# Rows 1 to 3 of Wo split in steps 6, 10 and 15 of a group, and the last Q tile evicted behind the transposes of P

## The chip, the cores and the metric

The kernel runs on one core of a Trainium2 chip. The metric is the device time of one execution in microseconds (us). TensorE is called PE here, VectorE DVE, ScalarE ACT, GpSimd POOL and SyncE SP; SP only issues DMAs.

## What is computed

The reference is one gated cross-attention layer and one gated feed-forward layer over 16 batches of 128 tokens of width 1024, in float32:

```python
q = (layernorm(x) @ Wq)                      # 32 heads of 32
k, v = ctx_4096 @ Wk, ctx_4096 @ Wv          # 8 heads of 32, 4 query heads share one
attn = softmax(q k^T / sqrt(32))
x = x + tanh(g_xattn) * ((attn v) @ Wo)
x = x + tanh(g_ffn) * (silu(layernorm(x) @ W_gate.T) * (layernorm(x) @ W_up.T)) @ W_down.T
```

## The kernel before

Every large product is made of three matmuls on 32-bit operands: each operand is split into a high part, which ACT writes by a rounding copy (L730), and a low part, the difference, which DVE writes (L1059). Weights, P, Q and the attention output all go through such a pair, ACT first and DVE behind it.

The attention works in 4 groups (g) of 4 batches, 512 tokens each. Within a group a program order is written out by hand in steps n = 0 to 37; in the first 32 of them (UNITS = 32) there is one unit of scores each: the scores of one batch and four heads. The steps are not synchronised; they only give the order of each engine's queue. In step n:

- PE (L1618 to L1644) makes the scores of unit n, one quarter of a Q tile (`q_part(n + 2)`, 6 matmuls, while n < 22; the 8 Q tiles are i = 0 to 7, and tile 7 is finished in step 21), the transposes of P of unit n - 3, from step 22 to step 29 one part of the output product with Wo (`o_part`), and in even steps from 6 on the product of P with V of pair m = (n - 6) / 2 (`weigh_values`, L1560), 12 matmuls.
- ACT (L805 to L820) evicts the output of pair m (`o_out`, odd n from 7, m = (n - 7) / 2), the transposed P of unit n - 3 (`pt_out`), computes the exponentials of unit n (`exps`, 4 activations), evicts a Q tile in steps 2, 6, 10, ..., 22 (`q_out`, two activations of 64 rows), and then copies the high part of a column tile of the weights (COL_STEP) or of a row of Wo (ROW_STEP), if one is due in this step.
- DVE (L1200 to L1218) takes the row maxima of unit n, inverts the sums of unit n - 1, makes the low part of a Q tile in steps 3, 7, ..., 23, the low part of the weights that ACT split one step before, the low part of the output of a pair (`o_out`), and the low part of P (`pt_out`).
- POOL multiplies P by the inverted sums (L624), and builds the block form of V (L594).
- SP (L377) issues the loads in an order of its own, each behind the wait for its buffer.

`weigh_values` of pair m waits for the low part of the output of pair m - 1 (`o_lo`, L1563 to L1564), since both use PSUM bank 5. The scores of units 24 and above read the last Q tiles: unit 25 is the first that needs tile 7, and so does `o_part(0, 3, 1)` in the same step, whose PSUM bank it was in.

A row of Wo goes through one buffer, `wr_raw`: SP loads row i once the low part of row i - 1 is made (`load_wr`, L340). Four rows (0 to 3) are ready before the output product of the group begins, rows 4 to 7 follow after the steps. `place_keys(g, 1, c)` (L360) is 12 DMAs of 32 KB that copy the keys of the second half of the heads into the block form `kb_h`, `kb_l`; c = 0 is needed by the scores of unit 16 (L1536), c = 1 by those of unit 20. In SP's queue `place_keys(g, 1, 0)` stands behind the loads of column tiles 8 and 9 (L386, L387), and the load of row 2 of Wo behind `place_keys(g, 1, 0)`.

After the attention come two halves of the feed-forward layer (from 700 us on), which the change does not touch.

Of the kernel before, what the change touches and what calls it, by code (L numbers as in the profile page):

```python
# [23 lines left out]
NQ = D // P  # L24
# [6 lines left out]
UNITS = NB * NH * GQ  # L31
# [3 lines left out]
STEPS = UNITS + 5  # L35

COL_STEP = {5: 0, 6: 5, 7: 9, 8: 32, 9: 33}
ROW_STEP = {0: 1, 1: 13, 2: 17, 3: 21}
KB_DMAS = 12 * 16


# [43 lines left out]
def gated_cross_attention_ffn(nc, x, ctx_t, wc, wr, wf, wm, wd, g_xattn, g_ffn, x1d, hd, out):  # L85

    with ExitStack() as ctx:
# [201 lines left out]
        def wcn(g, i):  # L289
            return g * NC + (NKV + i)  # L290
# [43 lines left out]
        def _(sp):  # L334
            def load_wc(g, i):

                sp.wait_ge(wc_lo, wcn(g, i) - 1)
                sp.dma_start(wc_raw[:, i % 2, :], wc[i]).then_inc(wc_in[i % 2], 16)

            def load_wr(g, i):  # L340

                if i > 0:
                    sp.wait_ge(wr_lo, g * NO + i)
                sp.dma_start(wr_raw[:, :], wr[i]).then_inc(wr_in, 16)
# [15 lines left out]
            def place_keys(g, a, c):  # L360
                if a == 0:
                    sp.wait_ge(kb_zero, g + 1)
                    sp.sem_inc(passed, 1)
                    sp.wait_ge(k_lo, g * NB + (2 * c + 2))
                else:
                    sp.wait_ge(s_done, g * UNITS + (8 + 4 * c + 4))
                two = slice(2 * c, 2 * c + 2)
                for j in range(4):
                    src, cols = slice(j * HD, (j + 1) * HD), slice(j * P, (j + 1) * P)
                    kl = kc_l[src, a, 2 * c * P:(2 * c + 2) * P].rearrange("p (b k) -> p b k", b=2)  # L370
                    kh = kc_h[src, a, 2 * c * P:(2 * c + 2) * P].rearrange("p (b k) -> p b k", b=2)
                    sp.dma_start(kb_l[src, two, cols].bitcast(F32), kl.bitcast(F32)).then_inc(kb_in[c], 16)
                    for half in range(2):
                        rows = slice(half * H2 + j % 2 * HD, half * H2 + j % 2 * HD + HD)
                        sp.dma_start(kb_h[rows, two, cols].bitcast(F32), kh.bitcast(F32)).then_inc(kb_in[c], 16)

            def body(g, last):  # L377
                load_wc(g, 4)
                load_wr(g, 0)
                load_wc(g, 5)  # L380
                place_keys(g, 0, 1)
                load_wc(g, 6)
                load_wr(g, 1)
                load_wc(g, 7)
                if not last:
                    load_wc(g, 8)  # L386
                    load_wc(g, 9)  # L387
                place_keys(g, 1, 0)
                load_wr(g, 2)
                place_keys(g, 1, 1)  # L390
                load_wr(g, 3)
                load_wr(g, 4)
                if last:
                    sp.wait_ge(wc_used, NG * NQ)
                    sp.wait_ge(x1_out, 16 * 8 + 1)
                    sp.dma_start(xa[:, :, :], x1d[0:NB].rearrange("t p n -> p t n")).then_inc(xa_in, 16)
                    sp.dma_start(xb[:, :, :], x1d[NB:2 * NB].rearrange("t p n -> p t n")).then_inc(xb_in, 16)
                    load_fraw(0, 0, 0)
                sp.wait_ge(pt_done, g * UNITS + UNITS)
                for i in (5, 6, 7):  # L400
                    sp.dma_start(wl_raw[:, :] if i == 7 else wo_raw[:, i - 5, :], wr[i]).then_inc(wo_in[i - 5], 16)
                if not last:
                    load_xn(g, 0)
                    load_xn(g, 1)
                    load_wc(g, 10)
                    load_wc(g, 11)
                sp.wait_ge(pv_done, g * PAIRS + PAIRS)
                if not last:
                    for b in range(2):
                        load_ct(g + 1, b, ctx_t[bass.ds(g * NB + (NB + b), 1), :, :].rearrange("o p n -> (o p) n"))  # L410
                src = x[g * NB:(g + 1) * NB] if last else x[bass.ds(g * NB, NB), :, :]
                sp.dma_start(x1[:, :, :], src.rearrange("t p n -> p t n")).then_inc(x1_in, 16)
                if not last:
                    for b in range(2, NB):
                        load_ct(g + 1, b, ctx_t[bass.ds(g * NB + (NB + b), 1), :, :].rearrange("o p n -> (o p) n"))
                if not last:
                    load_wc(g + 1, 0)
                    load_wc(g + 1, 1)
                for n, t in enumerate(LAST_ORDER if last else range(NB)):
                    sp.wait_ge(x1_add, g * YN + (2 * n + 2))  # L420
                    if not last and n in (1, 2):
                        load_xn(g, n + 1)
                    dst = x1d[g * NB + t] if last else x1d[bass.ds(g * NB + t, 1), :, :].rearrange("o p n -> (o p) n")
                    sp.dma_start(dst, x1[:, t, :]).then_inc(x1_out3 if last and t == NB - 1 else x1_out, 16)
                if not last:
                    load_wc(g + 1, 2)
                    load_wc(g + 1, 3)
# [142 lines left out]
            for g in range(NG - 1):  # L570
                body(g, False)
# [156 lines left out]
        def _(act):  # L728
# [69 lines left out]
            def body(g, last):  # L798
                kt_out(g, 3)
                split_wc(g, 4)  # L800
                q_out(g, 0)
                q_out(g, 1)

                act.wait_ge(x1_out, g * (16 * NB) + 1)
                for n in range(STEPS + 1):  # L805
                    if n >= 7 and n % 2 == 1:
                        o_out(g, (n - 7) // 2)
                    if 3 <= n < UNITS + 3:
                        pt_out(g, n - 3)
                    if n < UNITS:  # L810
                        exps(g, n)
                    if n % 4 == 2 and n < UNITS - 8:
                        q_out(g, n // 4 + 2)

                    for i in COL_STEP:
                        if COL_STEP[i] == n and not (last and i >= NQ):
                            split_wc(g, i)
                    for i in ROW_STEP:
                        if ROW_STEP[i] == n:
                            split_wr(g, i)  # L820

                for e in range(4):
                    act.wait_ge(o_first, g * 4 + (e + 1))
                    split_wr(g, 4 + e)
                if not last:
                    G = g + 1
                    split_wc(g, NQ + 2)
                    split_wc(g, NQ + 3)
                    split_ct(G, 0)
                    split_ct(G, 1)  # L830
                    kv_out(G, 0)
                    split_ct(G, 2)
                    split_wc(G, 0)
                    kv_out(G, 1)
                    split_ct(G, 3)
                    kt_out(G, 0)
                    xt_out(G, 0)
                    xt_out(G, 1)
                    split_wc(G, 1)
                    kv_out(G, 2)  # L840
                    kt_out(G, 1)
                    xt_out(G, 2)
                    xt_out(G, 3)
                    kv_out(G, 3)
                    kt_out(G, 2)
                    split_wc(G, 2)
                    split_wc(G, 3)
# [208 lines left out]
        def _(dve):  # L1056
# [136 lines left out]
            def body(g, last):  # L1193
# [6 lines left out]
                for n in range(STEPS + 1):  # L1200
                    if n < UNITS:
                        row_max(g, n)
                    if 1 <= n < UNITS + 1:
                        invert(g, n - 1)

                    if n % 4 == 3 and n < UNITS - 8:
                        q_out(g, n // 4 + 2)
                    for i in COL_STEP:
                        if COL_STEP[i] + 1 == n and not (last and i >= NQ):
                            split_wc(g, i)  # L1210
                    for i in ROW_STEP:
                        if ROW_STEP[i] + 1 == n:
                            split_wr(g, i)
                    if n >= 7 and n % 2 == 1:
                        m = (n - 7) // 2
                        o_out(g, m)
                    if 3 <= n < UNITS + 3:
                        pt_out(g, n - 3)  # L1218
                if last:
                    dve.wait_ge(rs2, 1)  # L1220
                    dve.wait_ge(xa_in, 16)
                    dve.wait_ge(xb_in, 16)
                    for t in range(NB - 1):
                        normalise_first(t)
# [688 lines left out]
```

## Time and profile before

| what | us |
|---|---|
| median of 3 runs | 2035.76 |
| lowest and highest of them | 2034.85 to 2037.85 |
| the profiled execution, its own time | 2039.46 |
| its span, first to last instruction | 2037.7 |
| attention, groups 0 to 3 with what lies before | 0 to about 700 |

The granted clock of TensorE is 0.997 of full speed over the span. Times of the trace are counted from the start of the span. A matmul in the trace has a modelled length that reaches over the start of the next one, so what a wait costs PE is read from the distance between starts. A row of the timeline gives start, length, engine, line, operation, output <- inputs and form; behind it stands the idle time before it and what ended that.

### The profile page before, as it was taken

The page shows a single profiled execution, that of the slowest core. Times are in us where ns is not written, and L with a number is a line of the kernel's source. Part 1 is how long each engine was busy: PE and PEld are TensorE (multiplying, and loading weights), DVE is VectorE, ACT ScalarE, POOL GpSimd, SP SyncE. Part 2 cuts the span into 40 slices and gives each one's busy share as a digit, 9 for nine tenths or more (in the row PEclk, how much of TensorE's full clock was granted, in tenths as well). Part 3 has the DMA queues.
Part 4 walks back from the last instruction along what each step waited for, and adds up shares of the span by engine and source line. Part 5 has one row for each costly group of instructions (what it writes and reads, how often), then busy time and mean ns, then how long its engine had stood idle before and what let it go on. Part 6 is the DMA issues. An engine that isn't in the chain of part 4 may idle for free.

```text
span 2037.7 us, 29091 instructions
## 1 busy us (share of the span) xinstructions
PE 1998.2 (98%) x9800; PEld 1677.5 (82%) x9800; DVE 1224.3 (60%) x1818; ACT 913.2 (45%) x2218; POOL 653.4 (32%) x601
## 2 busy tenths in 40 slices
PE   8999999999999999999999999999999999999999
PEld 6888888888888888888888878777888888888877
DVE  7767776776776864545543655574544545444455
ACT  4873683586387443333333434343333333233334
POOL 2440441242244554544542201023454454300000
PEclk9999999999999999999999999999999999999999
DMA  5225215324424222212213576763222222256676
GB/s 199 82 91 191 90 49 210 118 58 161 143 60 173 89 83 93 92 62 93 93 62 127 188 253 189 239 207 104 82 93 75 79 93 79 87 171 207 209 237 220
DMA packets 90634, 266.49 MB, mean 131 GB/s; under 512 B 11184, under 2 KB 37296, under 8 KB 85168
## 3 DMA queue, kind: packets, MB, share of 16 engines
q1 hardware_dynamic: 90256, 264.81, 38.8%
q8 instruction: 51, 0.84, 0.2%
q10 hardware_dynamic: 288, 0.52, 0.1%
q14 instruction: 39, 0.32, 0.0%
HBM read 221.25 MB, written 39.32 MB: 128 GB/s over the span
## 4 chain that ended last, share of the span: by engine, by line
PE 87%; DVE 7%; ACT 4%; issue 1%; DMA 0%; DVEq 0%; SPq 0%; ACTq 0%
PE ps L1507 27%; PE ps L1508 27%; PE ps L1509 27%; ACT pb L787 2%; PE ps L1557 2%; PE ps L1549 1%; PE ps L1548 1%; DVE wc_l L1059 1%; DVE qo_l L1095 1%; DVE qo_h L1095 1%; DVE kb_h L1109 1%; ACT wc_h L730 1%; DVE xo L1405 1%; PE ps L1602 1%; DVE dl L1059 1%
## 5 line engine op out<-in xcount | busy, mean ns | idle before, releaser
L1507 PE MATMUL ps<-xop_h,w_h 128*128 128x512 f32 x1208 | 473.2, 392 | 3.0 <-issue 3.0
L1508 PE MATMUL ps<-xop_l,w_h 128*128 128x512 f32 x1208 | 471.2, 390 | 0.0
L1509 PE MATMUL ps<-xop_h,w_l 128*128 128x512 f32 x1208 | 471.1, 390 | 0.0
L1507 PE MATMUL ps<-dh,hh 128*128 128x512 f32 x672 | 265.1, 394 | 6.3 <-DVE xo L1405 5.1
L1507 PEld LDWEIGHTS ps<-xop_h,w_h 128*128 128x128 f32 x1208 | 227.5, 188 | 50.3 <-issue 3.4
L1509 PEld LDWEIGHTS ps<-xop_h,w_l 128*128 128x128 f32 x1208 | 227.4, 188 | 47.3
L1508 PEld LDWEIGHTS ps<-xop_l,w_h 128*128 128x128 f32 x1208 | 227.5, 188 | 46.6
L1509 PE MATMUL ps<-dh,hl 128*128 128x512 f32 x672 | 261.9, 390 | 0.0
L1508 PE MATMUL ps<-dl,hh 128*128 128x512 f32 x672 | 261.9, 390 | 0.0
L1059 DVE TENSOR_TENSOR w_l<-fraw,w_h 128x512 fp32r<-128x512 f32 x130 | 129.4, 996 | 213.5 <-ACT w_h L730 213.5
L730 ACT ACTIVATE w_h<-fs 128x512 fp32r<-128x512 f32 x168 | 105.7, 632 | 292.5 <-PE ps L1509 281.7
L1059 DVE TENSOR_TENSOR dl<-dr,dh 128x1024 fp32r<-128x1024 f32 (+1 forms) x132 | 170.9, 1294 | 46.5 <-ACT dh L730 46.4
L624 POOL TENSOR_TENSOR pb<-pb,rinv 128x512 f32<-128x512 f32 x128 | 133.2, 1041 | 202.1 <-DVE rinv L1119 202.1
L787 ACT ACTIVATE pb<-ps,nmx 128x128 f32<-128x128 f32 x512 | 182.7, 389 | 18.3 <-DVE nmx L1114 17.8
L694 POOL TENSOR_TENSOR hb<-hb,cc 128x512 f32<-128x512 f32 x42 | 54.2, 1290 | 405.0 <-ACT hb L914 400.4
L730 ACT ACTIVATE hh<-hr 128x384 fp32r<-128x384 f32 (+1 forms) x132 | 64.5, 489 | 260.1 <-PE ps L1509 254.7
L1059 DVE TENSOR_TENSOR hl<-hr,hh 128x384 fp32r<-128x384 f32 (+1 forms) x126 | 72.2, 573 | 146.4 <-ACT hh L730 146.3
L1507 PEld LDWEIGHTS ps<-dh,hh 128*128 128x128 f32 x672 | 126.4, 188 | 35.0 <-DVE dl L1059 6.8
L1509 PEld LDWEIGHTS ps<-dh,hl 128*128 128x128 f32 x672 | 126.3, 188 | 26.5
L1508 PEld LDWEIGHTS ps<-dl,hh 128*128 128x128 f32 x672 | 126.4, 188 | 24.6
L730 ACT ACTIVATE dh<-dr 128x1024 fp32r<-128x1024 f32 x132 | 138.2, 1047 | 4.0 <-DMA dr<-in_wd 4.0
L1059 DVE TENSOR_TENSOR w_l<-fs,w_h 128x512 fp32r<-128x512 f32 x168 | 138.0, 823 | 1.6 <-ACT w_h L730 1.6
(161 smaller groups left out, 3856.3 us busy)
## 6 DMA issues: line engine op xcount, KB each, us to landing
dr<-in_wd SPq DMA_DIRECT2D x132, 512.0 KB, 4.3
fraw<-in_wf SPq DMA_DIRECT2D x42, 1024.0 KB, 5.4
wc_raw<-in_wc SPq DMA_DIRECT2D x44, 512.0 KB, 4.3
hd<-hb SPq DMA_DIRECT2D x42, 512.0 KB, 2.9
hr<-hd SPq DMA_DIRECT2D x84, 192.0 KB, 2.9
wr_raw<-in_wr SPq DMA_DIRECT2D x20, 512.0 KB, 3.6
x<-in_x SPq DMA_DIRECT2D x4, 2048.0 KB, 11.4
x1d<-x SPq DMA_DIRECT2D x16, 512.0 KB, 4.8
```

Source lines behind the costliest of these rows:

```text
L624: nc.gpsimd.tensor_tensor(p, p, r, ALU.mult).then_inc(normed, 1)
L694: nc.gpsimd.tensor_tensor(hb[:, 1, :], hb[:, 1, :], cc[:, 1, :], ALU.mult).then_inc(h_ready, 1)
L730: return nc.scalar.activation(out, in_, ACT.Copy, scale=scale)
L787: ins = nc.scalar.activation(pb[:, n % 4, j * P:(j + 1) * P], ps[:, n % 3, j * P:(j + 1) * P], ACT.Exp, bias=nmx[:, n % 4, j:j + 1], accum ...
L1059: return nc.vector.tensor_tensor(out, whole, hi.bitcast(F32), ALU.subtract)
L1095: ins = nc.vector.scalar_tensor_tensor(q[others, i, :], ps[rows, q_bank(i), :], SCALE, q[rows, i, :].bitcast(F32), ALU.mult, ALU.subtract)
L1109: ins = nc.vector.tensor_copy(kb_h[rows, b, cols], kc_h[src, 0, keys].bitcast(F32))
L1405: nc.vector.scalar_tensor_tensor(place, ps[:, Y_BANK[p][idx], :], tg[:, 1:2], place, ALU.mult, ALU.add).then_inc(y_free, 1)
L1507: pe.matmul(out, w_hi_, m_h, start=first, stop=False, skip_group_check=goes_on)
L1508: pe.matmul(out, w_hi_, m_l, start=False, stop=False, skip_group_check=goes_on)
L1509: return pe.matmul(out, w_lo_, m_h, start=False, stop=last, skip_group_check=goes_on)
L1557: ins = pe.transpose(ps[:, 3 + n % 2, j * P:(j + 1) * P], pb[:, n % 4, j * P:(j + 1) * P], ident[:, :])
```

## The change

Three things are moved; nothing is added or removed.

```diff
-ROW_STEP = {0: 1, 1: 13, 2: 17, 3: 21}
+ROW_STEP = {0: 1, 1: 6, 2: 10, 3: 15}
...                                          SP, body
                 load_wr(g, 1)
                 load_wc(g, 7)
+                load_wr(g, 2)
                 if not last:
                     load_wc(g, 8)
                     load_wc(g, 9)
+                load_wr(g, 3)
                 place_keys(g, 1, 0)
-                load_wr(g, 2)
                 place_keys(g, 1, 1)
-                load_wr(g, 3)
                 load_wr(g, 4)
...                                          ACT, step n
                     if 3 <= n < UNITS + 3:
                         pt_out(g, n - 3)
+                    if n == UNITS - 9:
+                        q_out(g, NQ - 1)
                     if n < UNITS:
                         exps(g, n)
-                    if n % 4 == 2 and n < UNITS - 8:
+                    if n % 4 == 2 and n < UNITS - 10:
                         q_out(g, n // 4 + 2)
...                                          DVE, step n
-                    if n % 4 == 3 and n < UNITS - 8:
+                    if n % 4 == 3 and n < UNITS - 9:
                         q_out(g, n // 4 + 2)
...
                     if 3 <= n < UNITS + 3:
                         pt_out(g, n - 3)
+                    if n == UNITS - 9:
+                        q_out(g, NQ - 1)
```

ACT splits the rows 1, 2, 3 in steps 6, 10, 15 and DVE makes their low parts in steps 7, 11, 16; before it was 13, 17, 21 and 14, 18, 22. Q tile 7 is evicted by ACT in step 23 between `pt_out` and `exps`, before it was the end of step 22; by DVE at the end of step 23, before it was ahead of `o_out` and `pt_out` of step 23. On SP the loads of rows 2 and 3 now stand ahead of `place_keys(g, 1, 0)`.

## Rows read from the trace of the kernel before

**Rows 1.** The page: busy time, share of the span, instructions

```profile
PE 1998.2 (98%) x9800; PEld 1677.5 (82%) x9800; DVE 1224.3 (60%) x1818; ACT 913.2 (45%) x2218; POOL 653.4 (32%) x601
```

**Rows 2.** Waits of PE (us in total, times, longest), whole span

```profile
PE ps L1507 <- DVE qo_l L1059: 9.4, 12, 1.4
```

**Rows 3.** Timeline of PE, end of steps 8 and 10 of group 1

```profile
242.49 0.60 PE L1557 MATMUL ps<-ident,pb 128*128 128x128 f32 x4
243.59 0.36 PE L1507 MATMUL ps<-pt_h,vp_h 128*128 128x256 f32 x1 [0.51 <-DVE qo_l L1059]
...
249.28 0.60 PE L1557 MATMUL ps<-ident,pb 128*128 128x128 f32 x4
249.63 0.36 PE L1507 MATMUL ps<-pt_h,vp_h 128*128 128x256 f32 x1
```

**Rows 4.** Timeline of DVE, step 7 of group 1

```profile
242.30 0.69 DVE L1095 SCALAR_TENSOR_TENSOR qo_l<-ps,qo_l 64x512 fp32r<-64x512 f32 x1
243.02 0.42 DVE L1059 TENSOR_TENSOR qo_l<-ps,qo_h 128x256 fp32r<-128x256 f32 x1
```

**Rows 5.** Timeline of ACT in step 9, DVE in 11, PE in 12, group 1

```profile
247.61 0.60 ACT L730 ACTIVATE pt_h<-ps 128x512 fp32r<-128x512 f32 x1 [1.15 <-PE ps L1557]
...
254.94 0.43 DVE L1059 TENSOR_TENSOR qo_l<-ps,qo_h 128x256 fp32r<-128x256 f32 x1
...
255.67 0.36 PE L1507 MATMUL ps<-pt_h,vp_h 128*128 128x256 f32 x1
```

**Rows 6.** DVE's low parts of rows 0 to 4: count, ns min/median/max

```profile
L1059 DVE TENSOR_TENSOR wr_l<-wr_raw,wr_h x20: 1226/1432/1980, 59.3 to 666.5; 128x1024 fp32r<-128x1024 f32 x20
```

**Rows 7.** Timeline of POOL and DVE in steps 3 and 7 of group 1

```profile
228.74 1.04 POOL L624 TENSOR_TENSOR pb<-pb,rinv 128x512 f32<-128x512 f32 x1 [1.84 <-DVE rinv L1119]
228.89 1.98 DVE L1059 TENSOR_TENSOR wr_l<-wr_raw,wr_h 128x1024 fp32r<-128x1024 f32 x1 [0.23 <-ACT wr_h L730]
...
241.49 1.04 POOL L624 TENSOR_TENSOR pb<-pb,rinv 128x512 f32<-128x512 f32 x1 [0.98 <-DVE rinv L1119]
```

**Rows 8.** Timeline of ACT and DVE, steps 21 to 23 of group 1

```profile
285.71 1.08 ACT L730 ACTIVATE wr_h<-wr_raw 128x1024 fp32r<-128x1024 f32 x1
286.66 0.62 ACT L730 ACTIVATE pt_h<-ps 128x512 fp32r<-128x512 f32 x1
...
288.50 0.61 ACT L730 ACTIVATE qo_h<-ps 64x512 fp32r<-64x512 f32 x1
289.74 0.38 ACT L730 ACTIVATE qo_h<-ps 128x256 fp32r<-128x256 f32 x1
...
289.75 0.68 DVE L1095 SCALAR_TENSOR_TENSOR qo_h<-ps,qo_h 64x512 fp32r<-64x512 f32 x1 [0.21 <-ACT qo_l L730]
291.17 0.42 DVE L1059 TENSOR_TENSOR qo_l<-ps,qo_h 128x256 fp32r<-128x256 f32 x1
```

**Rows 9.** Timeline of PE, step 24 and the start of 25, group 1

```profile
288.65 0.28 PE L1549 MATMUL ps<-kb_l,qo_l 128*128 128x256 f32 x1
289.00 0.63 PE L1557 MATMUL ps<-ident,pb 128*128 128x128 f32 x4
289.93 0.40 PE L1509 MATMUL ps<-wr_h,qo_l 128*128 128x512 f32 x1
291.74 0.36 PE L1507 MATMUL ps<-pt_h,vp_h 128*128 128x256 f32 x1 [1.41 <-DVE qo_l L1059]
293.24 0.28 PE L1548 MATMUL ps<-kb_h,qo_h 128*128 128x256 f32 x1
```

**Rows 10.** SP's issues before step 16, landing of `kb_h` (min/median/max), unit 16's scores

```profile
252.41 0.60 SPq L372 DMA_DIRECT2D kb_l<-kc_l  x1
258.80 1.24 SPq L375 DMA_DIRECT2D kb_h<-kc_h  x2
...
DMA to landing us min/median/max: 1.9/1.9/3.2
...
265.45 0.36 PE L1548 MATMUL ps<-kb_h,qo_h 128*128 128x256 f32 x1
```

## Prediction, made before the changed kernel was run

> **What bounds the kernel.** I read the page first, then the table of PE's waits, then PE's timeline by the distance between starts. The page shows PE busy for 98% of the span [rows 1]: the time is PE's queue plus the holes in it. Most work is feed-forward, which the change doesn't touch, so only holes of the attention can move. The waits show that in the attention PE has practically one releaser, DVE's `qo_l`, 12 times, 9.4 us [rows 2]: three places, the same in each of the four groups. They are:
>
> - Step 8, ahead of `weigh_values(1)`: from the start of the transposes to its first matmul it is 243.59 - 242.49 = 1.10 us, where step 10 has 249.63 - 249.28 = 0.35 [rows 3]. The hole is 0.75 us.
> - Step 24, ahead of `weigh_values(9)`: 291.74 - 289.93 = 1.81 us after the last matmul of `o_part`, whose successor comes 0.23 us later where nothing waits, so 1.58; in the same step the transposes come 0.35 us after the last matmul of the scores instead of 0.12, another 0.23 [rows 9]. Together 1.81 us.
> - Step 32, about half a microsecond: DVE's `o_out` stands there behind row maxima which wait for PE's own scores. It is tied to PE and moves with it; the change leaves it alone.
>
> **The change, part by part.** All times are those of group 1.
>
> *What goes: the hole of step 24.* In the old order ACT copies row 3 of Wo at 285.71, the last thing of step 21; the copy takes 0.95 us of ACT's queue (the next operation follows 0.95 us later), and so the exponentials of unit 22, and behind them Q tile 7 at 288.50, come late. DVE does this tile from 289.75 and only behind it the `o_out` of pair 8 at 291.17, whose end, 291.17 + 0.42 = 291.59, releases PE 0.15 us later at 291.74 [rows 8, 9]. The new order takes 0.95 us out of ACT ahead of it, and puts `o_out` and `pt_out` of step 23 ahead of the tile on both engines. ACT's `o_out(8)` then starts where the tile did, less the copy: 288.50 - 0.95 = 287.55. DVE makes it behind the row maxima of unit 23, which follow PE; it ends by about 288.9, and `weigh_values(9)`, without any hole due at 291.74 - 1.81 = 289.93, finds it done. The hole of 0.23 goes too: its transposes waited for a low part of P that stood behind the low part of row 3. Gain 1.81 us.
>
> What is late next is tile 7 itself. ACT: from 287.55 `o_out` and `pt_out`, 0.38 and 0.62 long; an ACT operation starts 0.13 before the end of the one ahead (285.71 + 1.08 against 286.66), so they take 0.74 and the tile is copied from 288.29, two halves in 1.24 (288.50 to 289.74) to 289.53. DVE: two halves in 1.42 (289.75 to 291.17) to 290.96, and PE could go on at 291.11. The scores of unit 25 are due 1.50 us (293.24 - 291.74) after `weigh_values(9)`, at 289.93 + 1.50 = 291.43 [rows 8, 9]. It fits by 0.32 us. This is the thinnest cover in the sum; if it were gone, each tenth of a microsecond beyond is one tenth lost per group.
>
> *What comes: row 1 in step 7 of DVE.* The low part of row 1 now stands between the Q tile of step 7 and `o_out(0)`, that is, directly ahead of the operation for which PE already waits in step 8. `o_out(0)` starts at 243.02, right behind the tile [rows 4]. ACT's copy of row 1, 1.08 long, starts when ACT has done its part of the Q tile, and so does DVE's part of the tile, which takes 1.42 [rows 8]: the copy is ready first and adds nothing. The shortest low part takes 1.226 us [rows 6]; the next operation starts 0.08 us before its end, so 1.15 us are put in. The hole of 0.75 becomes 1.90. The trace of before has no such split in this place. From below, it costs nothing if DVE had room there, which the rows exclude: the tile and `o_out` are back to back. From above, the longest of the 20 took 1.98 [rows 6], so 1.90. I take 1.15, since the long one at 228.89 began while POOL's multiply of 228.74 was running, whereas POOL's multiply of this step runs from 241.49 to 242.53 and is over before 243.02 [rows 7].
>
> The Trainium skill says why ("SBUF — State Buffer", section "Who interferes with whom"): a DVE instruction with two SBUF inputs and a GpSimd instruction that reads SBUF exclude each other, and the one that issues second blocks. The trace agrees: 228.74 + 1.04 + 1.23 = 231.01, the long split ended at 230.87. By this rule both new places are free of POOL; if one took the median of 1432 ns instead, the sum below would grow by 2 x 0.2 x 4 = 1.6 us.
>
> *Row 2 in step 11 of DVE.* The same order one period later: the low part stands between the Q tile and `o_out(2)`. That one started at 254.94, ended at 255.37 and would have let PE go at 255.52; `weigh_values(3)` started at 255.67 without a hole [rows 5]. So 0.15 of the 1.15 is covered and 1.00 is a new hole. Bounds: nothing, and 1.90 - 0.15 = 1.75; I take 1.00 for the same reason as above. By then the shift of step 8 has moved all queues alike: after each of these holes ACT and DVE stand ahead of PE again within two steps, because in step 9 of the old trace ACT sat idle for 1.15 us ahead of its `pt_out`, waiting for PE [rows 5], and likewise in step 13.
>
> *Row 3 in step 16 of DVE, rows 1 and 2 gone from 14 and 18.* Step 16 is even: behind the split come only `pt_out` and the next row maxima. The old order had the same split in steps 14 and 18, which are even too, and PE has no wait there [rows 2]. Nothing gained, nothing lost; from above, a split that meets POOL lasts 0.75 us more and still fits.
>
> *SP's queue.* The 12 DMAs of `place_keys(g, 1, 0)` started at 252.41 and the last was issued at 258.80 + 0.62 = 259.42, 7.01 us later [rows 10]. Now the load of row 3 stands ahead of them and waits for the low part of row 2. That ends, in old times plus the 1.15 of step 8, at 254.94 + 1.15 + 1.23 = 257.32. So: row 3 issued at 257.35, keys from 257.73, the last at 264.74, landed 1.9 us later at 266.64; with the longest landing of 3.2 at 267.94 [rows 10]. PE wants them at 265.45 + 1.15 + 1.00 = 267.60. Hidden by 0.96 us, in the worst case late by 0.34. `place_keys(g, 1, 1)` has no such gate and is needed four steps later. The loads of rows 2 and 3 themselves have over 6 us each until ACT wants them. In the last group row 4 and with it `x` for the feed-forward part are loaded sooner, but nothing reads them before the steps are over, so this is worth nothing.
>
> **Sum.** Per group +1.15 + 1.00 - 1.58 - 0.23 = +0.34 us, four groups +1.4 us. The profiled execution had a span of 2037.7 and a time of 2039.46; it would become 2039.1 and 2040.8. Its time lies 3.7 us above the median of the runs, so on the median: 2035.76 + 1.4 = 2037.1 us.
>
> **Rivals.**
>
> - *The new splits are hidden, and only the gain is seen:* -1.81 x 4 = -7.2, 2028.5 us. For it: DVE is busy only 60% of the span [rows 1], and ACT has idle time in step 9 [rows 5]. Against it: the releaser of the hole in step 8 is named, and the split stands directly ahead of it [rows 3, 4].
> - *POOL takes the splits:* if the low parts of rows 1 and 2 fall on POOL's multiply, each takes 1.98 as at 228.89, +1.90 + 1.75 - 1.81 = +1.84 per group, +7.4, 2043.1 us. It decides once DVE's split starts less than about 0.2 us after POOL's start; against it, 0.49 us lie between POOL's end and the split [rows 4, 7].
> - *The keys come late:* unit 16 of each group waits for a DMA. If the twelve issues take 0.6 us longer and land in 3.2, it is 0.34 + 0.6 = 0.94 per group, 3.8 in all, with the sum 2040.9 us. For it: a new gate ahead of the keys; against it: the median landing leaves 0.96 us [rows 10].
> - *Tile 7 is late:* the scores of unit 25 wait instead of `weigh_values(9)`. If it comes 0.7 us later than worked out, 0.37 per group, 1.5 in all, 2038.6 us.
>
> **How the numbers follow.** The forecast gets 0.50, the first rival 0.17, POOL 0.12, the keys 0.11, tile 7 0.10. The likeliest case and the last rival stay within 0.2% (4.1 us, about what a measurement of this kernel can tell from no change), as does a part of the keys' case, and those of partial cover on either side: faster 0.18, same 0.62, slower 0.20. The range reaches down towards the first rival and up to just short of POOL's: 2030.5 to 2042.5; the forecast's own is 2035 to 2039.5.
>
> **What would show it.** In the profile after: the wait of PE on `qo_l` in step 8 grows to about 1.7 us as listed (0.51 before), one of about 1 us appears in step 12, the one of 1.4 in step 24 is gone, the one of step 32 stays. The waits on `qo_l` are 12 again. DVE's `wr_l` of steps 7 and 11 take 1.23. SP's keys start 5 us later in the group, and PE lists no wait for a DMA of `kb_h`. The prediction is wrong if step 8 or 12 show no longer hole, if `wr_l` takes near 2 us there, or if unit 16 or unit 25 has a wait of its own.

## The result

| | before | after |
|---|---|---|
| median, 20 runs each | 2037.75 us | 2040.15 us |
| lowest to highest | 2034.85 to 2041.3 | 2038.66 to 2044.26 |
| profiled execution, its time and its span | 2039.46, 2037.7 | 2039.48, 2037.7 |

The ratio of the runs is 1.0017, 95% interval [1.0011, 1.0023]: the changed kernel is slower by 3.5 us, between 2.2 and 4.7; the two medians alone differ by 2.4. I had forecast 1.4 us more. The reader is to see three things in the profile after: both new holes are there, the old one is gone, and one of the rivals came true in one group of four. Engine busy times and PE's waits, from the page and the table of waits (us in total, times, longest):

```profile
PE 1995.8 (98%) x9800; PEld 1677.1 (82%) x9800; DVE 1228.0 (60%) x1818; ACT 914.0 (45%) x2218; POOL 649.1 (32%) x601
```

```profile
PE ps L1511 <- DVE qo_l L1061: 12.1, 12, 1.8
PE ps L1552 <- issue: 0.3, 1, 0.3
```

The waits on `qo_l` are 12 as in [rows 2], but 12.1 us instead of 9.4 (L1061 and L1511 are L1059 and L1507 of before). A second row has appeared, the scores' wait on nothing that the profile names.

Step 8 of group 1, PE's timeline, then DVE's of step 7:

```profile
243.37 0.60 PE L1561 MATMUL ps<-ident,pb 128*128 128x128 f32 x4
245.75 0.35 PE L1511 MATMUL ps<-pt_h,vp_h 128*128 128x256 f32 x1 [1.78 <-DVE qo_l L1061]
...
243.19 0.69 DVE L1097 SCALAR_TENSOR_TENSOR qo_l<-ps,qo_l 64x512 fp32r<-64x512 f32 x1
243.92 1.23 DVE L1061 TENSOR_TENSOR wr_l<-wr_raw,wr_h 128x1024 fp32r<-128x1024 f32 x1
245.18 0.42 DVE L1061 TENSOR_TENSOR qo_l<-ps,qo_h 128x256 fp32r<-128x256 f32 x1
```

The low part of row 1 stands between the Q tile and `o_out(0)`, and PE goes on 0.15 us after `o_out` ends (245.60). From the transposes to `weigh_values(1)` it is 2.38 us where [rows 3] had 1.10: 1.28 more. In step 11 and 12 the same picture, DVE first:

```profile
257.08 1.23 DVE L1061 TENSOR_TENSOR wr_l<-wr_raw,wr_h 128x1024 fp32r<-128x1024 f32 x1
258.34 0.42 DVE L1061 TENSOR_TENSOR qo_l<-ps,qo_h 128x256 fp32r<-128x256 f32 x1
...
258.91 0.35 PE L1511 MATMUL ps<-pt_h,vp_h 128*128 128x256 f32 x1 [0.85 <-DVE qo_l L1061]
```

From `weigh_values(1)` to `weigh_values(3)` it is 258.91 - 245.75 = 13.16 us, before 255.67 - 243.59 = 12.08 [rows 3, 5]: 1.08 more. Step 24 of PE, and Q tile 7 on DVE:

```profile
291.88 0.28 PE L1553 MATMUL ps<-kb_l,qo_l 128*128 128x256 f32 x1
292.00 0.60 PE L1561 MATMUL ps<-ident,pb 128*128 128x128 f32 x4
293.13 0.28 PE L1511 MATMUL ps<-pt_h,vp_h 128*128 128x256 f32 x1
294.56 0.28 PE L1552 MATMUL ps<-kb_h,qo_h 128*128 128x256 f32 x1
...
291.29 0.40 DVE L1061 TENSOR_TENSOR qo_l<-ps,qo_h 128x256 fp32r<-128x256 f32 x1
293.47 0.69 DVE L1097 SCALAR_TENSOR_TENSOR qo_l<-ps,qo_l 64x512 fp32r<-64x512 f32 x1
```

No hole is left: from the last matmul of the scores of unit 24 to the first of unit 25 it is 2.68 us, before 293.24 - 288.65 = 4.59 [rows 9], a gain of 1.91. `o_out(8)` is done at 291.69, well ahead. Tile 7 ends at 294.16, so PE could go on at 294.31, and the scores begin at 294.56: it fits by 0.25 us.

A period of a group, from the wait of step 32 in group 1 to that in group 2, sums it up; the row of each kernel, before and then after:

```profile
308.40 0.36 PE L1507 MATMUL ps<-pt_h,vp_h 128*128 128x256 f32 x1 [0.40 <-DVE qo_l L1059]
478.01 0.36 PE L1507 MATMUL ps<-pt_h,vp_h 128*128 128x256 f32 x1 [0.40 <-DVE qo_l L1059]
```

```profile
309.70 0.36 PE L1511 MATMUL ps<-pt_h,vp_h 128*128 128x256 f32 x1 [0.40 <-DVE qo_l L1061]
479.73 0.35 PE L1511 MATMUL ps<-pt_h,vp_h 128*128 128x256 f32 x1 [0.41 <-DVE qo_l L1061]
```

169.61 us became 170.03: 0.42 more (1.28 + 1.08 - 1.91 = 0.45, the rest is rounding of starts).

**The keys.** In group 0, and only there, unit 16 waits. SP first, then PE:

```profile
87.76 0.33 SPq L344 DMA_DIRECT2D wr_raw<-in_wr  x1
88.13 0.60 SPq L372 DMA_DIRECT2D kb_l<-kc_l  x1
94.54 2.17 SPq L375 DMA_DIRECT2D kb_h<-kc_h  x2
...
97.75 0.60 PE L1561 MATMUL ps<-ident,pb 128*128 128x128 f32 x4
98.66 0.35 PE L1552 MATMUL ps<-kb_h,qo_h 128*128 128x256 f32 x1 [0.31 <-issue]
```

The keys start behind the load of row 3, at 88.13, and the last pair of issues takes 2.17 us where all pairs ahead of it take 1.24. The scores come 0.91 us after the transposes instead of 0.35: 0.56 us lost. The profile calls it "issue", not DMA; that it is the keys is shown below. The pair is one issue of 1.53 us, at 94.54, and one of 0.60, at 96.11. The second, the last that unit 16 needs, also landed later than its like, 2.5 us after its issue. Of that DMA alone:

```profile
DMA to landing us min/median/max: 2.5/2.5/2.5
```

The last one in group 1 was issued at 265.76 and took 1.9. The scores were due at 97.75 + 0.35 = 98.10. By these numbers, with the long issue alone the last key would have landed at 96.11 + 1.9 = 98.0, just in time; both together made the wait.

**Why the two profiled spans are equal.** Four groups at 0.42 and 0.56 for the keys are 2.2 us, yet both spans are 2037.7. The stretches show it (length, busy of each engine, PEclk, DMA): before, then after.

```profile
584.00:596.00 12.00, 12.00 (x81) 10.75 (x81) 9.07 (x18) 10.59 (x42) 5.63 (x9) 1.00 0.07 18
1300.00:1400.00 100.00, 91.66 (x393) 73.69 (x392) 65.74 (x80) 42.89 (x66) 18.91 (x12) 0.95 0.59 200
```

```profile
584.00:596.00 12.00, 10.22 (x60) 9.32 (x60) 7.71 (x14) 8.81 (x40) 4.38 (x7) 0.86 0.16 45
1300.00:1400.00 100.00, 92.44 (x409) 74.65 (x408) 69.35 (x83) 43.87 (x68) 19.39 (x12) 0.98 0.62 208
```

The granted clock fell to its lower level, 1.2 GHz, for short stretches in both (a granted share of 0.50 from 1382 to 1384 before, and from 588 to 590 after): before only between 1300 and 1400, after there for a shorter time and once between 584 and 596. By these shares full clock would have given back about (1 - 0.95) x 100 = 5 us before, and (1 - 0.86) x 12 + (1 - 0.98) x 100 = 3.7 us after. The distances between starts say where it went. Two instructions of DVE that both kernels have, one behind the attention and one behind 1400, before and then after:

```profile
743.51 0.69 DVE L1322 TENSOR_TENSOR cc<-ps,x1c 128x512 f32<-128x512 f32 x1 [1.29 <-PE ps L1509]
1421.35 0.69 DVE L1322 TENSOR_TENSOR cc<-ps,x1c 128x512 f32<-128x512 f32 x1 [1.29 <-PE ps L1509]
```

```profile
747.12 0.69 DVE L1326 TENSOR_TENSOR cc<-ps,x1c 128x512 f32<-128x512 f32 x1 [1.29 <-PE ps L1513]
1421.37 0.69 DVE L1326 TENSOR_TENSOR cc<-ps,x1c 128x512 f32<-128x512 f32 x1 [1.29 <-PE ps L1513]
```

Behind the attention the changed kernel is 3.61 us late, and behind 1400 it is 0.02 us late. Of the 3.61, 1.5 are the low clock in group 3: its period, from the wait of step 32 in group 2 to that in group 3, is 1.90 us longer than before (651.22 - 479.73 against 647.60 - 478.01), the period shown above only 0.42. So 2.1 us are the change, and the feed-forward part, which the change does not touch, gave back 3.6 where the clock was low for longer before (by the shares 5 - 2 = 3 of them). One pair of profiles can't settle a change of this size by its spans; the distances between starts in stretches at full clock can.

### The profile page after: what moved, and what is told of

The parts are those of the page before. It is cut to its first block, busy times and chain, and to the rows that moved or that the text cites. A ratio compares the mean times of both kernels' runs of the same rounds, so it can differ in the third digit from the quotient of the medians.

```text
span 2037.7 us, 29091 instructions
## 1 busy us (share of the span) xinstructions
PE 1995.8 (98%) x9800; PEld 1677.1 (82%) x9800; DVE 1228.0 (60%) x1818; ACT 914.0 (45%) x2218; POOL 649.1 (32%) x601
## 4 chain that ended last, share of the span: by engine, by line
PE 86%; DVE 7%; ACT 4%; issue 1%; DMA 0%; DVEq 0%; SPq 0%; ACTq 0%
PE ps L1511 27%; PE ps L1513 27%; PE ps L1512 27%; ACT pb L787 2%; PE ps L1561 2%; PE ps L1552 1%; PE ps L1553 1%; DVE wr_l L1061 1%; DVE qo_l L1097 1%; DVE qo_h L1097 1%; ACT wc_h L730 1%; DVE wc_l L1061 1%; DVE kb_h L1111 1%; DVE xo L1409 1%; PE ps L1606 1%
## 5 line engine op out<-in xcount | busy, mean ns | idle before, releaser
L1511 PE MATMUL ps<-xop_h,w_h 128*128 128x512 f32 x1208 | 472.5, 391 | 2.2 <-issue 2.2
L1511 PE MATMUL ps<-dh,hh 128*128 128x512 f32 x672 | 264.7, 394 | 6.4 <-DVE xo L1409 5.1
L1511 PEld LDWEIGHTS ps<-xop_h,w_h 128*128 128x128 f32 x1208 | 227.2, 188 | 49.3 <-issue 2.6
L1061 DVE TENSOR_TENSOR w_l<-fraw,w_h 128x512 fp32r<-128x512 f32 x130 | 130.2, 1001 | 212.7 <-ACT w_h L730 212.7
L1061 DVE TENSOR_TENSOR dl<-dr,dh 128x1024 fp32r<-128x1024 f32 (+1 forms) x132 | 170.8, 1294 | 48.5 <-ACT dh L730 48.4
L1061 DVE TENSOR_TENSOR hl<-hr,hh 128x384 fp32r<-128x384 f32 (+1 forms) x126 | 72.1, 572 | 144.6 <-ACT hh L730 144.5
L1511 PEld LDWEIGHTS ps<-dh,hh 128*128 128x128 f32 x672 | 126.2, 188 | 34.9 <-DVE dl L1061 6.9
L1061 DVE TENSOR_TENSOR w_l<-fs,w_h 128x512 fp32r<-128x512 f32 x168 | 138.5, 826 | 1.6 <-ACT w_h L730 1.5
```

Of the source, the lines that this page charges most:

```text
L1061: return nc.vector.tensor_tensor(out, whole, hi.bitcast(F32), ALU.subtract)
L1511: pe.matmul(out, w_hi_, m_h, start=first, stop=False, skip_group_check=goes_on)
```

## The experiments

All seven vary the place of the splits, of the Q tiles or of SP's load; the computation stays whole. The period is that of group 1 to 2 as above; its difference times four stands beside the measured medians. It is a rough measure, since the groups of one kernel differ (in e3 the three periods are 168.82, 169.39 and 169.02). The last column is better: the start of the DVE instruction behind the attention shown above (743.51 before), less that of before. No kernel but the changed one had low clock ahead of it; there the 1.5 us of group 3 are in it.

| kernel | median, and that of before beside it | ratio [95%] | period | 4 x difference | end of attention |
|---|---|---|---|---|---|
| changed kernel | 2040.15, 2037.75 | 1.0017 [1.0011, 1.0023] | 170.03 | +1.7 | +3.6, less 1.5 |
| e1_q_only | 2034.65, 2038.09 | 0.9981 [0.9972, 0.999] | 168.42 | -4.8 | -5.2 |
| e2_rows_only | 2044.93, 2038.09 | 1.0035 [1.0022, 1.0049] | 171.00 | +5.6 | +6.7 |
| e3_dve_order | 2036.44, 2038.09 | 0.9996 [0.9987, 1.0005] | 169.39 | -0.9 | -0.5 |
| e4_dve_order_keys | 2030.95, 2038.09 | 0.9968 [0.9956, 0.998] | 167.57 | -8.2 | -7.2 |
| e5_rows_even | 2028.91, 2037.21 | 0.9965 [0.9952, 0.9977] | 167.72 | -7.6 | -8.4 |
| e6_q_late | 2026.91, 2037.21 | 0.9949 [0.9935, 0.9962] | 166.93 | -10.7 | -10.6 |
| e7_keys_first | 2039.8 (one run), 2037.21 | | 169.80 | +0.8 | +0.9 |

**e1_q_only: the Q tile alone.** The kernel before with:

```diff
 ACT, step n, and likewise at the end of DVE's step
+                    if n == UNITS - 9:
+                        q_out(g, NQ - 1)
-                    if n % 4 == 2 and n < UNITS - 8:
+                    if n % 4 == 2 and n < UNITS - 10:
```

> The kernel before with only the eviction of Q tile 7 moved (ACT step 23 between pt_out and exps, DVE end of step 23); rows of Wo and SP's queue as before. Theory (DVE's order sets the holes): the hole of 1.58 us ahead of weigh_values(9) in step 24 goes, the 0.23 ahead of the transposes stays since row 3 is still split in steps 21/22, and tile 7 comes about 0.4 us too late for the scores of unit 25. Per group -1.58 + 0.4 = -1.2, in all -4.7 us against before. Holes of steps 8 and 12: 0.6 and 0. Rival (the copy of row 3 on ACT is what makes the hole): no gain, within 1 us of before.

It gained 3.4 us by the medians, 4.8 by the period. PE in steps 24 and 25 of group 1:

```profile
287.17 0.28 PE L1553 MATMUL ps<-kb_l,qo_l 128*128 128x256 f32 x1
287.52 0.63 PE L1561 MATMUL ps<-ident,pb 128*128 128x128 f32 x4
288.68 0.29 PE L1511 MATMUL ps<-pt_h,vp_h 128*128 128x256 f32 x1
290.46 0.39 PE L1552 MATMUL ps<-kb_h,qo_h 128*128 128x256 f32 x1 [0.18 <-DVE qo_l L1097]
```

The hole ahead of `weigh_values(9)` is gone, the transposes still come 0.35 us after the scores as in [rows 9], and there is a new wait on tile 7, which shows 1.78 us between `weigh_values` and the scores instead of 1.43 after: 0.35 us, expected 0.4. So the hole of 0.23 stays with the rows in their old places, and goes where they are moved (changed kernel and e2); that it is row 3 among them, in steps 21 and 22, is read from its place in the queues. The wait of 0.35 is tile 7's.

**e2_rows_only: the rows alone.** The changed kernel with the tile put back.

```diff
-                    if n == UNITS - 9:
-                        q_out(g, NQ - 1)
-                    if n % 4 == 2 and n < UNITS - 10:
+                    if n % 4 == 2 and n < UNITS - 8:
```

> The changed kernel with the Q tile left where it was before (rows in steps 6, 10, 15 and SP's new order only). Theory: the new holes of steps 8 (1.9) and 12 (0.97) are there as in the changed kernel; in step 24 the transposes have no hole, and the hole ahead of weigh_values(9) shrinks from 1.58 to about 0.85, since ACT has 0.95 less ahead of the tile. Per group +1.28 + 0.97 - 0.23 - 0.73 = +1.3, with 0.5 for the keys in group 0: +5.7 us against before. Rival (moving the tile brings nothing, the rows did all): same time as the changed kernel, +2 to +3.5 us.

Slower by 6.8 us by the medians, 5.6 by the period. The waits of PE (whole span), and step 24:

```profile
PE ps L1507 <- DVE qo_l L1059: 15.0, 16, 1.8
```

```profile
294.53 0.40 PE L1509 MATMUL ps<-wr_h,qo_l 128*128 128x512 f32 x1
295.66 0.36 PE L1507 MATMUL ps<-pt_h,vp_h 128*128 128x256 f32 x1 [0.72 <-DVE qo_l L1059]
```

Four waits per group now. The hole of step 24 is 295.66 - 294.53 - 0.23 = 0.90, expected 0.85. The new places of the rows are a loss on the whole, though they save 0.91 of the 1.81 us of step 24 by themselves (0.68 ahead of `weigh_values(9)` and the 0.23); the tile's move saves the rest.

**e3_dve_order: the same work, another place in DVE's step.**

```diff
 DVE, step n
-                    for i in ROW_STEP:
-                        if ROW_STEP[i] + 1 == n:
-                            split_wr(g, i)
                     if n >= 7 and n % 2 == 1:
                         o_out(g, m)
                     if 3 <= n < UNITS + 3:
                         pt_out(g, n - 3)
                     if n == UNITS - 9:
                         q_out(g, NQ - 1)
+                    for i in ROW_STEP:
+                        if ROW_STEP[i] + 1 == n:
+                            split_wr(g, i)
```

> The changed kernel with DVE's low part of the row put behind o_out and pt_out of its step. Theory (only the place in DVE's queue costs): hole of step 8 back to 0.6, hole of step 12 gone, step 24 without a hole: -7.2 us against before, but the row 2 low part now ends about 1 us nearer to the keys' deadline in PE's time, so unit 16 waits for the keys in every group, 1 to 1.5 us each, 1 more in group 0: -7.2 + 5 to 7 = between -2.5 and 0 us against before, with waits of PE in step 16. Rival (the amount of work that ACT and DVE have early in the group costs, wherever it stands): holes of steps 8 and 12 as in the changed kernel, +2 to +3.5 us.

The hole of step 12 is gone and that of step 8 is back near its size of before (0.98 us from the transposes in group 1, 1.18 to 1.19 in the others, against 1.10), and the gain went into a new one. PE's waits, step 16 of PE, and SP, group 1:

```profile
PE ps L1552 <- DVE qo_l L1097: 5.2, 4, 1.7
PE ps L1511 <- DVE qo_l L1061: 3.8, 8, 0.6
```

```profile
266.06 0.60 PE L1561 MATMUL ps<-ident,pb 128*128 128x128 f32 x4
267.70 0.36 PE L1552 MATMUL ps<-kb_h,qo_h 128*128 128x256 f32 x1 [1.04 <-DVE qo_l L1097]
...
258.33 0.33 SPq L344 DMA_DIRECT2D wr_raw<-in_wr  x1
265.10 1.24 SPq L375 DMA_DIRECT2D kb_h<-kc_h  x2
```

Unit 16 waits in every group. The table names DVE's `qo_l` of L1097, the Q tile; but the tile that unit 16 reads (4) is evicted in step 11 and was long done, and the last key was issued at 265.10 + 0.64 = 265.74, 1.96 us ahead of the scores: the landing time of [rows 10]. Here a wait for two semaphores is put down to the engine, and it was the DMA.

**e4_dve_order_keys.** As e3, and

```diff
-                load_wr(g, 3)
                 place_keys(g, 1, 0)
+                load_wr(g, 3)
                 place_keys(g, 1, 1)
```

> As e3_dve_order, and SP's load of row 3 put back behind place_keys(g, 1, 0). Theory: no wait in step 16, hole of step 8 at 0.6, none in steps 12 and 24: -1.81 x 4 = -7.2 us against before. The difference to e3_dve_order is the price of the gate ahead of the keys, 5 to 7 us. Rival (keys never matter): same time as e3_dve_order.

7.1 us faster than before by the medians. The row on L1552 is gone from the waits, which shows the reading of e3 to be right: nothing but SP's order differs. What is left of PE's waits on `qo_l`:

```profile
PE ps L1511 <- DVE qo_l L1061: 3.7, 8, 0.6
```

The gate cost 7.2 - 0.5 = 6.7 us by the end of the attention, (169.39 - 167.57) x 4 = 7.3 by the period, 5.5 by the medians.

**e5_rows_even.** The changed kernel with

```diff
-ROW_STEP = {0: 1, 1: 6, 2: 10, 3: 15}
+ROW_STEP = {0: 1, 1: 7, 2: 11, 3: 15}
```

and SP's order of e4.

> The changed kernel with rows 1, 2, 3 in ACT's steps 7, 11, 15 (DVE's 8, 12, 16, the even steps, in which no o_out follows) and the load of row 3 behind place_keys(g, 1, 0); DVE's order within a step as in the changed kernel. Theory: an even step hides the split as well as the place behind o_out does: hole of step 8 about 0.6, none in steps 12, 16 and 24, -7 us against before, the same as e4_dve_order_keys. Rival (DVE and ACT have too little room in steps 8 to 12, wherever the split stands): holes ahead of the transposes or the scores of steps 9 to 13, and less than half of the gain.

8.3 us faster. PE's waits on `qo_l` are nearly those of e4:

```profile
PE ps L1511 <- DVE qo_l L1061: 3.8, 8, 0.5
```

One step later is enough, without any other order in DVE's steps: DVE has room for the split in the even step, where no `o_out` stands behind it, and none ahead of `o_out` in the odd one.

**e6_q_late.** As e5, and all Q tiles from 2 on as tile 7 (ACT's step is shown; DVE makes its part of them at the end of the same step):

```diff
-                    if n == UNITS - 9:
-                        q_out(g, NQ - 1)
+                    if n % 4 == 3 and n <= UNITS - 9:
+                        q_out(g, n // 4 + 2)
                     if n < UNITS:
                         exps(g, n)
-                    if n % 4 == 2 and n < UNITS - 10:
-                        q_out(g, n // 4 + 2)
```

> As e5_rows_even, and every Q tile from 2 on evicted as tile 7 is: ACT in step 3, 7, 11, ... between pt_out and exps, DVE at the end of that step. Theory: the remaining hole of step 8 is DVE's Q tile standing ahead of o_out(0); it goes, -0.6 x 4 more: -9.5 us against before, with only the half microsecond of step 32 left per group. Rival (the hole is ACT's or PE's own chain): same time as e5_rows_even. It could also make the scores wait for a late tile, in step 9 first, as in e1_q_only's step 25.

10.3 us faster than before, ratio 0.9949 [0.9935, 0.9962]: the best of all, and better than both kernels. The waits, and steps 7 and 8 of DVE and PE in group 1:

```profile
PE ps L1507 <- DVE qo_l L1059: 1.7, 4, 0.4
```

```profile
238.71 0.38 DVE L1059 TENSOR_TENSOR qo_l<-ps,qo_h 128x256 fp32r<-128x256 f32 x1
239.93 0.68 DVE L1095 SCALAR_TENSOR_TENSOR qo_h<-ps,qo_h 64x512 fp32r<-64x512 f32 x1 [0.23 <-ACT qo_l L730]
...
239.88 0.60 PE L1557 MATMUL ps<-ident,pb 128*128 128x128 f32 x4
240.23 0.36 PE L1507 MATMUL ps<-pt_h,vp_h 128*128 128x256 f32 x1
```

`weigh_values(1)` follows the transposes by 0.35 us, for the first time without a hole. Only step 32 is left, four waits of 0.4.

**e7_keys_first.** The changed kernel with SP's order of e4 and nothing else.

> The changed kernel with nothing but SP's load of row 3 put back behind place_keys(g, 1, 0). Theory: the hole ahead of unit 16 in group 0 (0.4 to 0.55 us in the profile of the changed kernel) is the keys' landing and goes; holes of steps 8 and 12 stay at 1.9 and 0.97. Time: 0.5 us less than the changed kernel, which one run can't tell. Rival (something of group 0's own): the hole stays.

The wait on "issue" is gone and `qo_l` has its 12 waits:

```profile
PE ps L1511 <- DVE qo_l L1061: 11.5, 12, 1.8
```

So it was the keys. Not expected: in groups 1 to 3 the hole of step 8 is 0.2 us shorter than in the changed kernel, and the period with it (169.80). Similar shifts of 0.2 show in e1, e3 and e4 between groups. They go with the head of the group: where the hole is the shorter one, DVE's first row maxima start 0.85 to 0.87 us after the group's first scores, and 1.13 to 1.17 where it is the longer one (eight groups against twelve in the changed kernel, e1, e3, e4 and e7). In the changed kernel it is 1.14 or 1.15 in all four. What sets DVE back by these 0.3 us ahead of the steps is open.

## Why the prediction was right, step by step

- *The time:* forecast a median of 2037.1, measured 2040.15, 3.0 more. Of these 2.0 are the kernel before itself, whose three runs had the median 2035.76 and whose twenty have 2037.75; 1.0 is the change, 2.4 by the medians where 1.4 were forecast.
- *What bounds:* right. The three places of [rows 2] moved as said, step 32 stayed (0.40 as listed, before and after).
- *Step 24:* forecast -1.81, measured -1.91. The extra 0.1 goes with the hole: the matmul behind a wait has its successor 0.20 us later (291.94 - 291.74 in the kernel before) where it is 0.12 without a wait. Tile 7 was said to fit by 0.32 and fits by 0.25.
- *Row 1 in step 7:* forecast +1.15, measured +1.28. The term was mis-sized in one detail: I let `o_out` start 0.08 us before the end of the split, and it starts 0.03 us behind it (243.92 + 1.23 = 245.15, start 245.18), as behind the Q tile. That is 0.11 of the 0.13.
- *Row 2 in step 11:* forecast +1.00, measured +1.08, for the same reason.
- *POOL:* the two splits took 1.23 us each as argued, in all four groups. The one of step 16 met POOL and took 1.71, which cost nothing, as forecast. It started 0.41 us after POOL's multiply and was still 0.48 us longer than alone, so a split meets POOL also beyond the 0.2 us that the rival gave for the full 1.98:

```profile
271.52 1.04 POOL L624 TENSOR_TENSOR pb<-pb,rinv 128x512 f32<-128x512 f32 x1 [2.49 <-DVE rinv L1121]
271.93 1.71 DVE L1061 TENSOR_TENSOR wr_l<-wr_raw,wr_h 128x1024 fp32r<-128x1024 f32 x1 [0.49 <-ACT wr_h L730]
```

271.52 + 1.04 + 1.23 = 273.79, it ended at 273.64. By the Trainium skill's rule ("SBUF — State Buffer", section "Who interferes with whom") the second to issue blocks until the first is done; the trace agrees within 0.15 us, as at [rows 7].

- *The keys:* forecast as hidden by 0.96 us, late by 0.34 at worst. In groups 1 to 3 hidden, in group 1 by 268.68 - 265.76 - 1.9 = 1.0, as forecast; in group 0 late by 0.56, because one issue of SP took 0.93 us longer than its like and the last DMA landed after 2.5 us instead of 1.9. The prediction had both in this rival (0.6 for the issues, a landing of 3.2). It named a wait of unit 16 as a sign of being wrong, and in one group of four it was. e3 shows how near it was in the others: there PE came to unit 16 earlier, and waited 1.3 to 1.7 us in each of groups 1 to 3.
- *The sum:* forecast +0.34 per group and +1.4 in all; by the periods it is +0.42 per group, with the keys +2.2 in all, by the end of the attention +2.1. That is near the 2.4 of the medians and the lower end of what the ratio gives (2.2 to 4.7); whatever the runs have beyond it is not explained by the trace. The sum per group came out within 0.1 partly because its errors have both signs: the losses were larger by 0.21, the gain by 0.10.

The rival by which only the gain is seen fell with e2: the rows' new places cost 1.39 us per group, after what they save in step 24. The POOL rival fell with the 1.23 us, that of tile 7 with the 0.25 us that are left.

## What to carry to other kernels

In a program order written out by hand, a piece of work that is "free" on an engine busy 60% of the time is free only where no operation for which the bottleneck waits stands behind it; the same split of 1.23 us cost 1.1 to 1.3 us ahead of `o_out` and nothing behind it (e4) or one step later (e5). Each hole that is closed brings the next deadline nearer: e3 closed 7.2 us and lost 6.7 to DMAs whose gate the change had moved. Put loads with a late gate behind transfers that have a deadline.

## What the runs showed of the hardware that was not expected

One issue of a 32 KB DMA in a pair took 0.93 us longer than its usual 0.60 (1.53 at 94.54 in the changed kernel), without any wait listed, and the next DMA, the last one before a deadline, landed after 2.5 us instead of 1.9. Why is open. In e2_rows_only the same place shows an issue of 1.10 and a landing of 2.4.

And the short falls of the granted clock, worth 3.7 and 5 us by their shares in the two profiles compared, lie at other places in each profile. All nine have at least one between 1300 and 1390; the changed kernel alone has one in the attention (587). So spans of two profiles differ or agree by more than the effect studied.
